# Second layer of a four-layer graph network: the left product is taken in the edge stage, and the dense stage adds gathered products to the right product

## The reference, cut to what matters

```python
# second layer, x: [10000, 512]
agg = segment_sum(x[src], dst, n)                 # sum of the sources' rows for each target
cnt = segment_sum(ones, dst, n)
mean_agg = agg / maximum(cnt, 1)[:, None]
h = mean_agg @ W_l.T + b_l + x @ W_r.T
h = (h - mean(h, axis=0)) * rsqrt(var(h, axis=0) + EPS) * gamma + beta
x = layernorm(x + relu(h) + x)
```

## Time and profile before

| | |
|---|---|
| median of 3 runs | 4138.68 us (4137.36 to 4145.64) |
| profiled execution, time | 4137.12 us |
| profiled execution, span | 4135.1 us, 57582 instructions |
| busy, share of the span | PE 86%, PEld 52%, DVE 51%, ACT 36%, POOL 36% |
| transfers | 800.08 MB, mean 193 GB/s |
| second layer: edge stage | from about 661 to 801 us |
| second layer: dense stage | from about 801 to 1312 us |

### The profile page before, as it was taken

How to read it: one execution, slowest core, us unless ns; L and a number is a source line. 1 busy time by engine, 2 the same in 40 slices (tenths; PEclk the granted TensorE clock), 3 DMA queues, 4 the chain that set the end, 5 groups by cost and what they waited for, 6 DMA issues and landing times. The chain is left out here.

```text
span 4135.1 us, 57582 instructions
## 1 busy us (share of the span) xinstructions
PE 3554.7 (86%) x20056; PEld 2138.1 (52%) x20056; DVE 2089.7 (51%) x3927; ACT 1479.1 (36%) x2584; POOL 1476.6 (36%) x1231
## 2 busy tenths in 40 slices
PE   4589994499997999988399999999777999948974
PEld 3134441255553777766266666666554555514543
DVE  7167775523332444437644343330566878605668
ACT  1333332322222444435233233332343344343357
POOL 2445543332221222235333333230436666434312
PEclk7789997699998999999699999999998999989985
DMA  1667776633343566549686766763777776466548
GB/s 67 211 181 198 199 183 203 214 127 129 122 131 113 194 220 217 209 168 279 203 229 198 202 201 200 207 176 89 211 216 265 264 265 254 163 216 201 176 162 276
DMA packets 533322, 800.08 MB, mean 193 GB/s; under 512 B 287494, under 2 KB 287494, under 8 KB 531152
## 3 DMA queue, kind: packets, MB, share of 16 engines
q1 hardware_dynamic: 466000, 577.37, 42.7%
q0 software_dynamic: 67200, 221.25, 18.5%
HBM read 470.83 MB, written 263.59 MB: 178 GB/s over the span
## 5 line engine op out<-in xcount | busy, mean ns | idle before, releaser
L325 PE MATMUL bank<-w_lo,t_r_hi 128*128 128x344 f16 (+1 forms) x2560 | 837.3, 327 | 0.0
L326 PE MATMUL bank<-w_hi,t_r_hi 128*128 128x344 f16 (+1 forms) x2560 | 837.1, 327 | 0.0
L324 PE MATMUL bank<-w_hi,w_lo 128*128 128x344 f16 (+1 forms) x1280 | 419.2, 327 | 30.9 <-DMA w_lo<-g_row_lo 30.9
L2250 DVE SCALAR_TENSOR_TENSOR t_z<-w_lo,t_z 128x256 f32<-128x256 f32 x320 | 209.2, 714 | 441.2 <-DMA w_lo<-h 438.5
L2224 POOL TENSOR_TENSOR t_row_lo<-t_r,t_row_hi 128x1024 f16<-128x1024 f32 x80 | 184.6, 2308 | 513.2 <-ACT t_row_hi L2271 513.0
L324 PE MATMUL bank<-l_z_hi,w_lo 128*128 128x512 f16 x960 | 364.4, 380 | 1.4 <-DVE l_z_lo L2633 1.4
L325 PE MATMUL bank<-l_z_lo,w_hi 128*128 128x512 f16 x960 | 364.3, 379 | 0.0
L326 PE MATMUL bank<-l_z_hi,w_hi 128*128 128x512 f16 x960 | 364.1, 379 | 0.0
L1463 POOL DMA_INDIRECT l_z<-sum,slot_i x160 | 165.9, 1037 | 484.1 <-PE bank L1833 284.8
L326 PEld LDWEIGHTS bank<-w_hi,t_r_hi 128*128 128x128 f16 x2560 | 250.9, 98 | 168.6 <-issue 0.8
L324 PE MATMUL bank<-w_hi 128*128 128x344 f16 x960 | 297.5, 310 | 45.8 <-DMA w_hi<-t_row_lo 45.8
(11 more groups left out here) (332 smaller groups left out, 7005.6 us busy)
## 6 DMA issues: line engine op xcount, KB each, us to landing
w_lo<-h SPq DMA_DIRECT2D x160, 512.0 KB
h<-b_wide SPq DMA_DIRECT2D x80, 516.0 KB, 2.9
h<-w_hi SPq DMA_DIRECT2D x80, 516.0 KB, 3.2
sum_gat<-a_out SPq DMA_DIRECT2D x80, 514.0 KB
l_x<-x SPq DMA_DIRECT2D x40, 1024.0 KB
sum<-e_out SPq DMA_DIRECT2D x120, 256.0 KB
g_x<-in_x SPq DMA_DIRECT2D x20, 1024.0 KB
x<-g_y SPq DMA_DIRECT2D x20, 1024.0 KB
```

What stands on the lines that cost most here:

```text
L324: pe.matmul(out, s_lo, m_hi, start=(k == 0), stop=False)
L325: pe.matmul(out, s_hi, m_lo, start=False, stop=False)
L326: mm = pe.matmul(out, s_hi, m_hi, start=False, stop=last)
L2250: ins = v.scalar_tensor_tensor(out=z[u][:, s, cols], in0=hrow[:, s, cols], scalar=z[u][:, s, HC + h:HC + h + 1], in1=z[u][:, s, cols], op0 ...
```

## The change

Each edge tile's scaled sum is multiplied by W_l right in the edge stage, so that the table `sum` holds products. A linear map commutes with gathering rows by target, so the dense stage needs only x1 @ W_r and adds the gathered products. In detail:

- A new `edge_product_stage` replaces the second layer's edge stage. After the f32 sum (`e_mean`, double buffered) PE turns the tile (4 blocks), ACT and DVE split it into f16 halves (`e_z_hi`, `e_z_lo`), PE multiplies it by W_l (12 matmuls of 512 columns), ACT takes it out of PSUM (`e_out`). Three tiles are in work at a time: PE's order is sum of tile t, turn of t-1, product of t-2.
- W_l is loaded in the kernel's first stage, third in line of `plain_weights`, which has three buffers there now; scratch that lay over W_l's place now begins at W_r's (`spare`).
- The other ten units of later weights (`LaterWeights`) are cut in pieces, one behind each tile's low part on DVE: `halves` (high and low part of one unit, both on DVE now) or one of four `logits` pieces (a product and a reduction). Loads are issued by SP between the tiles' stores.
- `sage_stage` replaces the dense stage of layer two: per group PE turns 4 chunks of x1 (for the next group), turns 4 chunks of the gathered products (`l_a`, L1985 of the changed kernel) into two banks of their own, and forms the four banks from 4 chunks each. ACT takes the product out with a scaled bias, DVE adds the turned gathered products from PSUM (L1947) and then takes the statistics. h stays scaled by 4096 (1/UNSCALE), and the coefficients' epsilon is scaled by its square. The stage is written out for 20 groups instead of a hardware loop.
- `rim_out` is dropped in favour of `e_first`; its transfer and its two DVE operations stay.

```diff
+class LaterWeights:
...
+    PIECES = 5
...
+        self.first = [n * self.PIECES for n in range(6)] + [31, 33, 35, 37]
...
+    def load(self, sp, n):
+        if n >= 2:
+            sp.wait_ge(self.lo_done.sem, self.lo_done.at(n - 1))
+            sp.wait_ge(self.wa_read.sem, self.wa_read.at(4 * min(n - 1, len(self.ATTENTION))))
+        sp.dma_start(self.stage_w[n % 2][:], self.kn.dram["weights"][self.units[n]]).then_inc(self.w_in[n % 2].sem, 16)
...
+        for n in range(2, len(self.units)):
+            before = self.first[n - 2] + (self.PIECES - 1 if n - 2 < len(self.ATTENTION) else 0)
+            if tile == before:
+                if self.units[n - 1] == W_GAT2:
+                    self.attention_row(sp, 1)
+                self.load(sp, n)
...
+    def piece(self, dve, tile):
+        for n, first in enumerate(self.first):
+            if tile == first:
+                self.halves(dve, n)
+            elif n < len(self.ATTENTION) and first < tile < first + self.PIECES:
+                self.logits(dve, n, tile - first - 1)
...
+def edge_product_stage(kn, mem):
...
+            weights.loads(sp, t)
+            sp.wait_ge(out_ready.sem, out_ready.at(t + 1))
+            sp.dma_start(dram["sum"][t * P:(t + 1) * P, :], out[o][:]).then_inc(kept[o].sem, 16)
...
+    def vector(dve):
+        v = nc.vector
+        for t in range(T):
+            u = t % 2
+            dve.wait_ge(hi_done.sem, hi_done.at(t + 1))
+            if t >= 2:
+                dve.wait_ge(prod.sem, prod.at(t - 1))
+            v.scalar_tensor_tensor(out=z_lo[u][:].rearrange("p k n -> p (k n)"), in0=tp[u][:], scalar=A_SCALE,
+                                   in1=z_hi[u][:].rearrange("p k n -> p (k n)"),
+                                   op0=ALU.mult, op1=ALU.subtract).then_inc(lo_done.sem, 1)
+            weights.piece(dve, t)
+        weights.finish(dve)
...
+        def take_mean(t):
+            act.wait_ge(summed.sem, summed.at(t + 1))
+            if t >= 2:
+                act.wait_ge(turned.sem, turned.at(t - 1))
+            act.activation(mean[t % 2][:], total[t % 2][:], ACT.Copy, scale=kn.mean_scale[:, t:t + 1])\
+               .then_inc(evacuated.sem, 1)
+        def high_part(t):
+            u = t % 2
+            act.wait_ge(turned.sem, turned.at(t + 1))
+            if t >= 2:
+                act.wait_ge(prod.sem, prod.at(t - 1))
+            act.activation(z_hi[u][:].rearrange("p k n -> p (k n)"), tp[u][:], ACT.Copy, scale=A_SCALE)\
+               .then_inc(hi_done.sem, 1)
+        def take_product(t):
+            o = t % O
+            act.wait_ge(prod.sem, prod.at(t + 1))
+            if t >= O:
+                act.wait_ge(kept[o].sem, kept[o].at(t // O * 48))
+            act.copy(out[o][:], mm[t % 2][:]).then_inc(out_ready.sem, 1)
+        for t in range(L - 1):
+            matrix(t)
+        for t in range(T + 2):
+            if t + L - 1 < T:
+                matrix(t + L - 1)
+            if t < T:
+                take_mean(t)
+            if 1 <= t <= T:
+                high_part(t - 1)
+            if t >= 2:
+                take_product(t - 2)
...
+        def sum_rows(t):
+            pe.wait_ge(lhs_ready.sem, lhs_ready.at(t + 1))
+            pe.wait_ge(gathered[t % W].sem, gathered[t % W].at(16 * (t // W + 1)))
+            if t >= 2:
+                pe.wait_ge(evacuated.sem, evacuated.at(t - 1))
+            pe.matmul(total[t % 2][:], lhs[t % L][:], rows[t % W][:], start=True, stop=True).then_inc(summed.sem, 1)
+        def turn(t):
+            u = t % 2
+            pe.wait_ge(evacuated.sem, evacuated.at(t + 1))
+            if t >= 2:
+                pe.wait_ge(lo_done.sem, lo_done.at(t - 1))
+            for k in range(4):
+                ins = pe.transpose(tp[u][:, k * P:(k + 1) * P], mean[u][:, k * P:(k + 1) * P], kn.ident[:])
+            ins.then_inc(turned.sem, 1)
+        def multiply(t):
+            u = t % 2
+            pe.wait_ge(lo_done.sem, lo_done.at(t + 1))
+            if t >= 2:
+                pe.wait_ge(out_ready.sem, out_ready.at(t - 1))
+            split_product(pe, mm[u][:], lambda k: (z_hi[u][:, k, :], z_lo[u][:, k, :]),
+                          lambda k: (kn.weights(False, W_SAGE_L, k), kn.weights(True, W_SAGE_L, k)), 4)\
+                .then_inc(prod.sem, 1)
+        for t in range(T + 2):
+            if t < T:
+                sum_rows(t)
+            if 1 <= t <= T:
+                turn(t - 1)
+            if t >= 2:
+                multiply(t - 2)
...
+        for g in range(G):
+            i, u = divmod(g, 2)
+            real = d.last_real if g == G - 1 else GROUP
+            for m in range(4):
+                if g + 1 < G:
+                    low_part(g + 1, m)
+                dve.wait_ge(a_turned.sem, a_turned.at(g * 4 + m + 1))
+                dve.wait_ge(biased.sem, biased.at(g * 4 + m + 1))
+                v.tensor_tensor(h[u][:, m, :], ta[m % 2][:], h[u][:, m, :], ALU.add).then_inc(h_done.sem, 1)
+                dve.wait_ge(h_done.sem, h_done.at(g * 4 + m + 1))
+                v.bn_stats(kn.bn_stats[:, m, g * 6:(g + 1) * 6], h[u][:, m, 0:real]).then_inc(seen.sem, 1)
...
+    def scalar(act):
+        def high_part(g, k):
+            act.wait_ge(turned.sem, turned.at(g * 4 + k + 1))
+            if g >= 2:
+                act.wait_ge(mid.sem, mid.at((g - 1) * 4))
+            act.activation(z_hi[g % 2][:, k, :], tp[k % 2][:], ACT.Copy, scale=A_SCALE).then_inc(hi_done.sem, 1)
+        for k in range(4):
+            high_part(0, k)
+        act.wait_ge(bias_ready.sem, bias_ready.at(1))
+        for g in range(G):
+            i, u = divmod(g, 2)
+            act.wait_ge(stored[u].sem, stored[u].at(i * 16))
+            for m in range(4):
+                if g + 1 < G:
+                    high_part(g + 1, m)
+                act.wait_ge(mid.sem, mid.at(g * 4 + m + 1))
+                act.activation(h[u][:, m, :], mm[m][:], ACT.Identity, bias=bias[:, m:m + 1]).then_inc(biased.sem, 1)
...
+        def turn_sums(g, m):
+            i, u = divmod(g, 2)
+            pe.wait_ge(sum_in[u].sem, sum_in[u].at(16 * S * (i + 1)))
+            pe.wait_ge(h_done.sem, h_done.at(g * 4 + m - 1))
             for s in range(S):
+                ins = pe.transpose(ta[m % 2][:, s * P:(s + 1) * P], a[u][:, s, m * P:(m + 1) * P], kn.ident[:])
...
+                if g + 1 < G:
+                    turn(g + 1, m)
+                turn_sums(g, m)
+                pe.wait_ge(biased.sem, biased.at((g - 1) * 4 + m + 1))
...
-        g.tensor_scalar(rstd[:], mv[:, :, 1], EPS, None, ALU.add).then_inc(steps.sem, 1)
+        g.tensor_scalar(rstd[:], mv[:, :, 1], EPS * scale * scale, None, ALU.add).then_inc(steps.sem, 1)
...
-            weights = plain_weights(kn, mem, list(range(W_SAGE_L)), 2)
+            weights = plain_weights(kn, mem, list(range(W_SAGE_L + 1)), 3)
...
-            plain = plain_weights(kn, mem, [W_SAGE_L, W_SAGE_R, W_FC, W_FC + 1, W_GCN], 2)
-            attention, beside = attention_weights(kn, mem)
-            kn.add(together(plain, attention,
-                            edge_sum_stage(kn, mem, dram["x1"], None, kn.mean_scale, kn.rim_mean_scale,
-                                           beside=beside)))
-        kn.add(linear_stage(kn, "sage"))
-        kn.add(norm_coefficients_stage(kn, V_SAGE_G, V_SAGE_BETA))
+            kn.add(edge_product_stage(kn, mem))
+        kn.add(sage_stage(kn))
+        kn.add(norm_coefficients_stage(kn, V_SAGE_G, V_SAGE_BETA, 1.0 / UNSCALE))
```

More of the change, by code:

```diff
@@ L233, in spare @@
             flat = flat.bitcast(dt)
[L234 removed]
+        assert at % 4 == 0 and first % 2 == 0 and at + n * size <= 2 * (UNITS * 4 * D + GAT_CHUNKS * LOGITS) - 2 * self.unit_at(W_SAGE_R)
         if len(shape) == 3:
@@ L1015, in sync @@
         sp.wait_ge(rim_ready.sem, rim_ready.at(2))
-        sp.dma_start(dram["sum"][d.rims:d.rims + T, :], rim_out[0:T, :]).then_inc(rim_kept.sem, 16)
+        sp.dma_start(dram["sum"][d.rims:d.rims + T, :], first[0:T, :]).then_inc(rim_kept.sem, 16)
         for o in range(O):
@@ L1664, in gin_stage, with sage_stage @@
     return {"sync": sync, "gpsimd": gpsimd, "vector": vector, "scalar": scalar, "tensor": tensor}
-def linear_stage(kn, layer):
+def sage_stage(kn):
     nc, d, dram, take, pair = kn.nc, kn.d, kn.dram, kn.sig.take, kn.sig.pair
-    G, H = d.groups, d.groups // 2
-    sage = layer == "sage"
-    chunks = 8 if sage else 4
-    unit = W_SAGE_L if sage else W_GCN
-    bias = V_SAGE_B if sage else V_GCN_B
-    x_dram = dram["x1"] if sage else dram["x3"]
-    turns = ((0, 1), (2, 3), (4, 5), (6, 7)) if sage else ((), (), (0, 1), (2, 3))
+    G, H, T = d.groups, d.groups // 2, d.tiles
     mem = ExitStack()
@@ L1684, in linear_stage @@
     x = two("l_x", [P, S, D], F32)
-    z = two("l_z", [P, S, D], F32)
-    z_hi = kn.buffer(mem, "l_z_hi", [P, 2, chunks, D], F16)
-    z_lo = kn.buffer(mem, "l_z_lo", [P, 2, chunks, D], F16)
+    a = two("l_a", [P, S, D], F32)
+    z_hi = two("l_z_hi", [P, 4, D], F16)
```

(21 more changed lines are left out.)

354 lines of the change are left out of this document (180 added, 174 removed).

## The result

The changed kernel takes 3969.53 us (median of 4 runs, 3968.99 to 3971.72), the kernel before 4138.02 us (4 runs, 4134.61 to 4145.64). The ratio is 0.9591, 95% interval 0.9575 to 0.9608: 168.5 us or 4.1% faster. The forecast was 3968 us. The profiled execution took 3969.53 us with a span of 3967.8.

The account below looks back on a forecast made before the run. PE was taken to bound the dense stage; in the edge stage no engine alone did. Dense -213.5, edge +40.1 and first stage +2.5 sum to -170.9 us, from 4137.1 to 3966.2, by the median 3968 us; range 3950 to 4010.

Parts of the forecast that it names:

- Dense stage, matmuls: Layer two's dense stage: 960 matmuls of 512 columns go, at 0.2155 us each, -206.9 us.
- Dense stage, borders: Dense stage group borders: PE waits for low parts, margin 0.3 us; 0.2 us per border taken, +4 us.
- Dense stage, opening and end: Dense stage: steady work 12.2 us after first issue instead of 23.7, -11.5 us; one DVE addition at the end, +0.9.
- Edge stage: Layer two's edge stage: 3.98 us per tile with the product, ending at 841.1 against 801.0, +40.1 us.
- the f32 sum: Edge stage, per tile on PE: 0.95 us taken, where four passes of 0.2155 would be 0.86.
- First stage: Kernel's first stage: W_l loaded ahead of the pairs delays the DVE chain, +2.5 us, bounds 0 to 4.0.
- The rest: Coefficients, batch norm and layer four's edge stage: same instructions, 0 us.
- 2 (transfers): Dense stage becomes bound by transfers at only 200 GB/s: +37 us, 4005 us; chance 9%.
- 3 (weight pieces hold tiles up): Edge stage: DVE waits for unlanded weight units, delaying low parts and PE: +25 us, 3993 us; chance 9%.
- 4 and 6 (clock stays low): PE's clock low in edge stage, +68, 4036 us, 6%; in both stages, slower than before, about 4150 us, 2%.
- 5: Turned blocks, 25% of dense-stage PE time, fail to keep the clock up: +88 us, 4056 us; chance 3%.

Follow-up runs that it names:

- the run of all three: Changed kernel with edge pairs loaded first, edge sums made turned at once, and weight loads held behind the first gather: 3945.58 us, ratio to before 0.9534.

## Why the prediction was right, step by step

- **Dense stage, matmuls.** Right (206.9, by bringing them back). The reasoning that carried it: the unit prices add up to the measured spacing of the banks at clock 1.00, so nothing waits, and unit price times count is time.
- **Dense stage, borders.** The margin was sized right, 0.33 us measured for 0.3, but I added 0.2 us of waiting per border on top of a positive margin. None came: -4 us. Pricing a positive margin as a cost belongs in the range, not in the sum. Against it stands a term that the sum lacks: sixteen turned blocks of the first group stood in the opening before and stand in steady work now, 16 x 0.11 = +1.8 us.
- **Dense stage, opening and end.** 12.2 us to steady work, as forecast, out of two errors of 0.6 us that cancel. From the last bias row to the next stage's first load it is 10.9 us for 9.7 before, +1.2 for +0.9. The opening scatters by 2 us with the moment at which PE's clock rises. Of the stage's -2.7 against the forecast some -0.8 us is left without a cause.
- **Edge stage, +36.1 for +40.1.** The term mis-sized is the f32 sum: 0.86 us by its columns was the lower bound in the text, and I took 0.95. Measured 3.885 per tile, -0.1 x 37 = -3.5. The end was 8.4 us for 9.7 (-1.3), from the last taking-out to the next load. Against both stands the first sum, 3.0 us late behind its gather's issue, as I had allowed too little for the loads beside it (1 for 4.1 us). All but 0.2 of it came back by the fourth sum's weight load at 678.17, with more of the opening's work at full clock than I had counted; that is luck. The last two tiles took 6.2 us for 5.6 (+0.6).
- **First stage, +2.5 for -0.6.** No step failed that the traces can name. The cause of the delay was right (`high_i` at 14.84 for 15.1), and it goes through the chain: at the seventh gather the eight traces of the changed order stand at 114.1 us on average, the three of before at 111.7. But the stage's time moves by more than the term from execution to execution: at layer two's first gather it is 659.2 to 664.1 us in these eight (mean 662.2) and 659.9 to 662.3 in the three (mean 661.4). So the -0.6 of one pair of traces says nothing against the term, the means say +0.8, and how much of the 2.4 us the stages up to there take back stays open. The mistake was to expect a term of 2.5 us to show in the difference of two traces.
- **The rest, +13.4 for 0.** "Same instructions, 0" failed in part. 3.6 us are the trace of before that was costed against, which lies under the mean of its three, 3.1 the trace after, which lies over the mean of the eleven (2828.2), and 6.7 the difference of the means, of which 2.5 are the recurring gap on DVE. This is why the total looks better than its terms, which is luck: -4.0, -3.1 and -2.7 in three terms, +13.4 in the fourth.
- **Rivals.** 2 (transfers) was refuted with room to spare, PE stayed full at 315 GB/s. 3 (weight pieces hold tiles up) didn't occur at 3.885 us per tile: DVE waited for no unit, and 1.8 us for a row of logit weights, which PE did not feel. With a shorter tile it shows: PE waits for low parts without the product, there because DVE is full and hardly because a unit is late (2.0 us), and in the run of all three behind late weights (2.7 and 1.3 us). 4 and 6 (clock stays low) did not occur: 1.00 from 674 us. 5: with turned blocks at 25% of PE's time, four took 0.44 us from start to start and the clock stayed at 1.00 for 272 us. The Trainium skill ("TensorE: Matmul & The Clock Gate", Part 4: PE-mode transpose) holds that transposes do not count as PE work the same way; at this share the trace shows no harm from it.

## What to carry to other kernels

Multiply on the side of a gather that has fewer rows, if the dense stage is bound by PE throughout: check that the unit prices add up to the measured spacing at full clock (the busy share alone hides short waits), and the gain is count times unit price. When a stage gains a product, look for the next engine in line (here DVE, a third of the product's work was paid in time) and for operand orders that make the transposing unnecessary. Cut both traces at the same marks and take several traces of both kernels: a term of 2 us can vanish in the difference of two traces, and a sum of small errors can hide behind a good total. Before a pair of traces is compared, see whether PE's clock rose at the same point of the work in both.

## What was not expected of the hardware

- A gap of 0.2 us on DVE between two operations of an unchanged, written-out stage, every eighth tile, in ten traces of eleven of the longer programs and in none of three of the shorter. 80 more DVE instructions ahead of it moved it from tiles 6, 14, 22 and 30 to 9, 17, 25 and 33. The untouched last 2285 us grew by 6.8 on average; most of that stays open.
- A gather of 128 rows took 3.5 us from issue to its consumer alone, and 7.6 beside three loads issued within the same microsecond.
- f32 matmuls of 128 moving columns with fresh 128x128 f32 weights each ran at 0.22 us per product, hardly above their column time.
- In the kernel's first stage the same 16 matmuls took 2.05, 2.40 and 3.76 us in three executions of the same program, since PE's clock rose at another moment; DVE waited 6.4, 6.7 and 8.4 us for that work, and the chain behind was 1.8 us later in the last.
